# Order of work in layers 1 and 2 of a four-layer attention and expert network on one Trainium2 core

## What is computed

```python
x = x + _L1_xattn_ref(_layernorm(x), ctx_768, ...)
x = x + _L1_ffn_ref(_layernorm(x), ...)
x = x + _L2_xattn_ref(_layernorm(x), ctx_768, ...)
x = x + _L2_ffn_ref(_layernorm(x), ...)

# layer 1, attention: every linear layer rounds its input to int8 steps (by the largest value of all of it)
for Wa, ba in ((W_att0, b_att0), (W_att1, b_att1)):
    kv = bitnet_linear(image_embeds, Wa, ba)
    k = jnp.concatenate([kv, kv], axis=-1)
    scores = jnp.einsum('bse,bpe->bsp', fused, k) * inv_sqrt_e
    attn = jax.nn.softmax(scores, axis=-1)
    fused = fused + 0.1 * jnp.einsum('bsp,bpe->bse', attn, k)
h = jax.nn.relu(bitnet_linear(concatenated, W_f1, b_f1))
return bitnet_linear(h, W_f2, b_f2)

# layer 1, experts
x_attn = _layernorm(x_flat, ln_g, ln_b) @ attn_w + attn_b + x_flat
h = jax.nn.gelu(jnp.einsum('metd,edf->metf', g, w1) + b1[None, :, None, :], approximate=False)
y = jnp.einsum('metf,efd->metd', h, w2) + b2[None, :, None, :]
out = jax.nn.gelu(y @ next_w + next_b, approximate=False)

# layer 2, feed-forward, twice (forward and inverse branch)
prod = xV * jnp.cumsum(yW, axis=1)
weights = jax.nn.softmax(logits, axis=-1)
out = jnp.einsum('btkr,kdr->btd', prod * weights[..., None], U)
```

## Time and profile before

| | |
|---|---|
| median of 3 runs | 1381.35 us (1381.34 to 1382.42) |
| profiled execution | 1381.36 us, span 1379.6 us |
| TensorE busy | 1333.7 us, 97% of the span |
| VectorE, ScalarE, GpSimd busy | 975.0, 944.9, 734.8 us |
| DMA | 20.59 MB, mean 15 GB/s |

### The profile page before, as it was taken

How to read it: one execution, slowest core, us unless ns; L and a number is a source line. 1 busy time by engine, 2 the same in 40 slices (tenths; PEclk the granted TensorE clock), 3 DMA queues, 4 the chain that set the end, 5 groups by cost and what they waited for, 6 DMA issues and landing times. The chain is left out here.

```text
span 1379.6 us, 30536 instructions
## 1 busy us (share of the span) xinstructions
PE 1333.7 (97%) x10001; PEld 992.9 (72%) x10001; DVE 975.0 (71%) x2367; ACT 944.9 (68%) x1964; POOL 734.8 (53%) x787
## 2 busy tenths in 40 slices
PE   8999999998988899999999999999999999999998
PEld 6555568996556777777775787677777777777777
DVE  6776757868767677777775565777766767677783
ACT  6888877885776476766763465676766767676673
POOL 6465641204532167666657486465665656565652
PEclk9999999999999999999999999999999999999999
DMA  6300010000003100000001000000000000000003
GB/s 180 88 0 0 1 31 2 1 1 1 2 1 96 47 1 1 1 0 0 0 1 39 0 1 0 1 2 1 1 0 0 0 0 0 0 0 0 1 3 91
DMA packets 31539, 20.59 MB, mean 15 GB/s; under 512 B 9589, under 2 KB 29020, under 8 KB 31452
## 3 DMA queue, kind: packets, MB, share of 16 engines
q1 hardware_dynamic: 31224, 19.38, 5.0%
q10 hardware_dynamic: 228, 0.10, 0.0%
HBM read 18.42 MB, written 1.05 MB: 14 GB/s over the span
## 5 line engine op out<-in xcount | busy, mean ns | idle before, releaser
L2410 POOL TENSOR_TENSOR arena<-arena,l3a_rinv 128x512 f32<-128x512 f32 x256 | 259.1, 1040 | 189.1 <-DVE l3a_rinv L2822 188.8
L2713 ACT ACTIVATE arena<-l3a_scores_ps,l3a_nmax 128x512 f32<-128x512 f32 x256 | 174.9, 686 | 116.0 <-DVE l3a_nmax L2816 115.9
L2410 POOL TENSOR_TENSOR arena<-arena,l2a_rinv 128x512 f32<-128x512 f32 x128 | 129.7, 1040 | 84.9 <-DVE l2a_rinv L2822 84.2
L2816 DVE TENSOR_REDUCE l3a_nmax<-l3a_scores_ps 128x2 f32<-128x1024 f32 x128 | 155.9, 1218 | 17.7 <-PE l3a_scores_ps L2483 17.7
L904 ACT ACTIVATE l0a_prob<-l0a_scores_ps,l0a_k_scale 128x1024 f32<-128x1024 f32 x128 | 135.5, 1114 | 21.8 <-PE l0a_scores_ps L749 20.4
L2713 ACT ACTIVATE arena<-l2a_scores_ps,l2a_nmax 128x512 f32<-128x512 f32 x128 | 87.5, 686 | 57.2 <-DVE l2a_nmax L2816 57.2
L2514 PE MATMUL l3a_work_ps<-l3a_probT,l3a_v 128*64 128x256 f32 x1024 | 124.6, 385 | 0.0
L2514 PEld LDWEIGHTS l3a_work_ps<-l3a_probT,l3a_v 128*64 128x64 f32 x1024 | 67.8, 136 | 48.7 <-issue 20.0
L2816 DVE TENSOR_REDUCE l2a_nmax<-l2a_scores_ps 128x2 f32<-128x1024 f32 x64 | 77.7, 1217 | 7.4 <-PE l2a_scores_ps L2483 7.4
L2828 DVE COPY l3a_probT<-l3a_scores_ps 128x512 f32<-128x512 f32 x65 | 44.9, 690 | 44.2 <-PE l3a_scores_ps L2491 44.1
L2828 DVE COPY l3a_probT<-l3a_work_ps 128x512 f32<-128x512 f32 x63 | 43.6, 691 | 36.7 <-PE l3a_work_ps L2491 35.9
(11 more groups left out here) (805 smaller groups left out, 3731.5 us busy)
## 6 DMA issues: line engine op xcount, KB each, us to landing
l1f_w<-in_L_ffn_w SPq DMA_DIRECT2D x16, 256.0 KB, 2.8
arena<-in_ctx SPq DMA_DIRECT2D x4, 384.0 KB, 5.2
w_l_w<-in_L_ffn_W SPq DMA_DIRECT2D x1, 1024.0 KB
arena<-in_L_ffn_W SPq DMA_DIRECT2D x16, 64.0 KB, 1.9
out_x<-x_tokens SPq DMA_DIRECT2D x8, 128.0 KB, 1.9
x_tokens<-in_x SPq DMA_DIRECT2D x1, 768.0 KB, 5.9
const<-in_constants SPq DMA_DIRECT2D x1, 525.0 KB
w_l_wo<-in_L_xattn_Wo SPq DMA_DIRECT2D x1, 512.0 KB
```

The source lines that it names most:

```text
L2410: e.tensor_tensor(prob[n][:, :], prob[n][:, :], bcast(rinv[:, n:n + 1], [P, S]), ALU.mult).then_inc(m.prob_ready, 1)
L2713: e.activation(prob[at][:, :], scores_bank(b, c, u), ACT.Exp, bias=nmax[:, at:at + 1], accum_out=rsum[:, at:at + 1]).then_inc(m.exp_ready, 1)
L2816: e.tensor_reduce(nmax[:, at:at + 2], sps[:, first:first + 1024].rearrange("p (h k) -> p h k", h=2), AX.X, ALU.max, negate=True).then_inc( ...
```

## The change

Nine pieces, all of them changes of order, of waits or of the number of fillers:

- attention of layer 1: project(n+2) stands ahead of scores(n+1) in every slot from 0 on; the final projections stand behind the transposes; at the end attended(15) stands ahead of the final of batch 6; VectorE's keep_rows(1) stands ahead of the division of step 0;
- experts of layer 1: apply(0) stands ahead of quantise(2) and quantise(3); turn_z and mix wait for each tile singly; in the last turn keep_y(3, 0) stands behind update(2) and the statistics;
- layer 2: 17 fillers for 8 ahead of the softmax's transposes and 1 for 4 ahead of the last of them; norm_scales at step 5 for step 6.

```diff
@@ l1_ffn, tensor @@
             def turn_z(u):
-                e.wait_ge(m.z_ready, NT * (u + 1))
...
                 for i in range(NT):
+                    e.wait_ge(m.z_ready, NT * u + i + 1)
                     last = e.transpose(turn_ps[:, i * P:(i + 1) * P], z[u % 2][:, i, :], g.ident)
...
-                e.wait_ge(m.inner_ready, NT * (u + 1))
                 for i in range(NT):
+                    e.wait_ge(m.inner_ready, NT * u + i + 1)
                     e.matmul(mix_ps[:, i * P:(i + 1) * P], inner[u % 2][:, i, :], g.ident, start=i == 0, stop=False)
@@ l1_ffn, vector @@
             statistics(0)
+            apply(0)
             quantise(2)
             quantise(3)
-            apply(0)
...
-                keep_y(u, 0)
+                if u < TURNS - 1:
+                    keep_y(u, 0)
                 if u >= 1:
                     update(u - 1)
                     ahead.statistics(e, u - 1, next_tiles(u - 1), m.x_updated, PAIR * u)
+                if u == TURNS - 1:
+                    keep_y(u, 0)
@@ l2_ffn, tensor @@
-                keep_busy(e, g, zps, 8)
+                keep_busy(e, g, zps, 17)
...
                     if n == TURNS - 1:
-                        keep_busy(e, g, zps, 4)
+                        keep_busy(e, g, zps, 1)
@@ l2_ffn, gpsimd @@
-                        if n == 6 and u > 0:
+                        if n == 5 and u > 0:
                             norm_scales(u - 1)
@@ l1_attention, vector @@
+                    if n == -1:
+                        keep_rows(n + 2)
                     if n + 1 < STEPS:
                         invert(n + 1, 0)
-                    if n + 2 < STEPS:
+                    if n >= 0 and n + 2 < STEPS:
                         keep_rows(n + 2)
@@ l1_attention, tensor @@
                 def slot(n):
+                    if n >= 0 and n + 2 < STEPS:
+                        project(n + 2)
                     if n == 0:
-                        project(n + 2)
                         project_sum(1, 0)
                     if n + 1 < STEPS:
                         scores(n + 1)
-                    if 0 != n < STEPS - 2:
+                    if n < 0:
                         project(n + 2)
...
-                    for b in range(B):
-                        if final_slot(b) == n:
-                            final(b, 2 + sum(SUM_AT[u] <= n for u in range(2, B // 2)))
                     if n >= 0:
                         turned(n, 0)
                         turned(n, 1)
+                    for b in range(B):
+                        if final_slot(b) == n:
+                            final(b, 2 + sum(SUM_AT[u] <= n for u in range(2, B // 2)))
                     if n >= 1:
                         attended(n - 1)
...
+                attended(STEPS - 1)
                 final(B - 2, B // 2)
-                attended(STEPS - 1)
                 final(B - 1, B // 2)
```

6 lines of the change are left out of this document (3 added, 3 removed).

## The result

The changed kernel takes 1385.78 us in the median of 9 runs (1384.90 to 1387.63), the kernel before 1382.24 us in the median of 9 (1381.34 to 1384.72). The ratio is 1.0020 with a 95% interval from 1.0011 to 1.0028: the change makes the kernel slower, by 1.5 to 3.9 us. The medians lie 3.5 apart. The forecast was +1.8 us, at 1383.2; its range reached to 1386.4. The sign came out as forecast and so did the main mechanisms; the size was put too low, by about half if the medians are taken.

What follows compares the result with a forecast made beforehand. TensorE, busy nearly throughout, was taken as the bound, so only its idle time and clock count. Terms -0.4 + 3.9 - 0.5 + 0.9 - 2.1 = +1.8 on 1381.36 gave 1383.2 us, range 1379.4 to 1386.4.

Steps and rivals of the forecast that it cites:

- Start of the layer-1 experts: apply(0) ahead of two quantisings: turn_z 3.3 us late, +2.8 net, plus 1.1 for a lower clock; together +3.9.
- Rival 1: Clock stays at 1.2 GHz after the 4.6 us hole in layer-1 experts: term 5.3, sum +3.2, about 1384.8; chance 0.24.
- Layer 2, norm scales: Layer-2 experts, scales a step sooner: +1.05 in turn 1, +0.9 in turn 2, -1.1 in turn 3; together +0.9.
- Rival 3: Layer-2 term a gain: GpSimd works ahead, only turn 3 shows, -1.1 for +0.9; 1381.2, no change; chance 0.10.
- Softmax fillers: Layer-2 softmax: with no idle hole the clock stays at 2.4 GHz, -2.1; -1.0 if it falls all the same.
- Experts' end: Layer-1 experts' end: update and statistics slide into VectorE's idle hole, products' copy and transposes come sooner; -0.5.
- Attention: Layer-1 attention, all its moves together: -0.4, bounds -3.1 without the port's effect and +0.5 if late steps cost more.
- four long steps: Attention steps whose projection waits for VectorE's quantising beside GpSimd's division: 4.66 us each, +3.6 together.
- seven short steps: Attention steps with the projection first, its copy ready early: 3.50 us, 0.25 gained in each, -1.8 together.
- tail's swap: Attention's end, attended(15) ahead of final(6): swaps one short wait for another, -0.2 at most.
- Rival 2: Faster: VectorE and GpSimd run ahead, late quantisings do not hold attention's scores; attention -3.7, about 1378.5; chance 0.13.
- Rival 4: Changes in order do nothing visible, each move lying under a busy engine; 1381.4; chance 0.08.

Runs made afterwards that it cites:

- run 4: Kernel before with only the softmax fillers changed, 17 for 8 and 1 for 4; 1381.51 us, ratio 0.9986 against the kernel before.
- run 12: Kernel before, unchanged, profiled a second time; span 1382.7 us against 1379.6 in its first profile.
- run 5: Changed kernel with VectorE's quantising of image rows of batches 3 to 7 moved right behind the two maxima; 1382.09 us, ratio 0.9993 against the kernel before.
- Run 1: Changed kernel with apply(0) of the layer-1 experts put back behind quantise(2) and quantise(3); 1381.09 us, ratio 0.9990 against the kernel before.
- run 7: Changed kernel with turn_z(0) and mix(0) ahead of second_product(2) and (3), and fourteen fillers ahead of turn_z; 1383.86 us, ratio 1.0006 against the kernel before.
- run 3: Changed kernel with layer 2's norm scales at step 6 again; 1384.87 us, ratio 1.0013 against the kernel before.
- run 8: Changed kernel with the edits of Run 1 and run 2, and norm scales sooner in the last turn alone; 1376.39 us, ratio 0.9955 against the kernel before.
- run 2: Changed kernel with layer-1 attention's projections put back behind the scores; 1382.65 us, ratio 0.9995 against the kernel before.
- run 9: As run 8, but projections ahead of scores, quantising as in run 5, final of batch 6 ahead of attended(15); 1374.77 us, ratio 0.9940 against the kernel before.
- run 6: Changed kernel with quantising and shifting of image rows of batches 4 to 7 a slot sooner; 1385.29 us, ratio 1.0015 against the kernel before.

## Why the prediction came out as it did

**How the total came about.** Against the profile that the sum was made from, the change measured +3.5 for +1.8. Attention missed by +1.7, the end of the experts by +0.9, layer 2 by +0.3; the start of the experts by -0.8 and the softmax by -0.1 took some of it back, and the stages that the change does not touch gave -0.3. That the total stayed within the range owes something to misses of both signs.

**Start of the layer-1 experts, +3.9: right, and the largest term.** turn_z late by 3.3 less what mix had waited was the working, with +2.8; against starts of 11.98 (runs 4 and 12, the old order at full clock) the changed kernel's 15.88 is +3.9. turn_z itself went from 7.91 (run 12) to 12.46 after the stage's start, 4.6, of which 1.3 is the clock. Against the one profile that the sum was made from the term is +3.12, because that profile had a lower clock in the very same stretch, which the working did not take out. Behind the hole the batch products took 1.89 instead of 1.22 and the fillers 1.64 instead of 1.03: 1.3 for the clock, 1.1 was taken. Rival 1, the same course with the clock low for longer, put the term at 5.3. The profile of run 5, with this order too, comes near it: 17.05, +5.1, with the granted clock at 0.53 and 0.50 from 424.0 to 430.8, through the batch products, the fillers, turn_z and most of mix, though not the first hidden product. Both courses happen, in different executions: the five profiles with this order have 15.88, 16.31, 16.33, 16.98 and 17.05, so +3.9 to +5.1 (three of them with the clock low at the stage's start as well), and the forecast stood at their lower end. Run 1 shows that the order causes it, run 7 that it is TensorE's order against VectorE's. GpSimd's first power took 1.03 instead of 1.47 without the quantising beside it, as the working had read.

**Layer 2, norm scales, +0.9: right in each turn.** Forecast +1.05, +0.9 and -1.1; measured waits +1.00, +0.92 and -0.91, and the stage +1.22, for a sum of waits of +1.01; the other 0.2 was not traced. Rival 3, that GpSimd works ahead, falls by run 3, and run 8 has the last turn alone at -0.80, so turns 1 and 2 cost 2.0.

**Softmax fillers, -2.1: right** with 2.24, shown by run 4 with this piece alone.

**Experts' end, -0.5: right** in the stretch that it named (-0.51), wrong in what came next. "The next late thing is ScalarE's last gelu" left out the five fillers, which at a lower clock become the last thing themselves: +0.95. Run 1, with the same edit and 1.28 for the fillers, shows that it belongs to the execution, not to the edit.

**Attention, -0.4: here the sum failed;** measured +1.26, the other way. The mechanism held: four long steps of 4.73 to 4.76 (forecast 4.66), four projections waiting on quantised rows, the start -1.20 (-1.2), the hole's step -0.71 (-0.8). Four sizes were off, all one way. The long steps came to 19.01 against 15.06 of the same steps before, +3.95 for +3.6. The seven short steps became 3.54 or 3.55, the last of them 3.48, where 3.50 was taken: -1.5 for -1.8. Two steps with a final grew from 4.06 to 4.21, +0.3, which the working had at nothing; run 2 has them at 4.09, so most of it is the projection. And the tail's swap, put at "-0.2 at most", cost +0.4: run 9. "One short wait for another" was said there without adding up the chain; a bound above zero was missing. The stated upper bound for attention, +0.5, was passed.

**Slips of arithmetic in the record**, none of them large: 4 x 4.66 less 15.1 is +3.5, not +3.6; the upper bound for attention comes to +0.4; rival 1's +3.2 gives 1384.6, not 1384.8.

**Rival 2** (VectorE and GpSimd run ahead, the quantisings do not hold) falls: with the change four projections wait for quantised rows, 4.4 us in all, and without their move (run 2) or with the quantising elsewhere (run 5) the long steps go. **Rival 4** falls with the table.

**The argument on the clock was weak.** "After 1.92 of idle it fell, after the 2.36 hole it did not" was read as a property of the two holes; run 12 shows the 2.36 hole with a fall. One profile shows one draw. The time of the kernel before was also read from its luckiest side: 1381.36 was among the fastest of what became nine runs with a median of 1382.24. Taken against that median the forecast rise of 1.8 would have stood at 1384.0, with 1385.78 measured. The ratio came out right at the bound of 0.2%, beyond which the forecast had given 0.33.

How much of a run's time is this draw can be read from the mean granted clock of each timing. Of 30 timings of the kernel before beside runs 1 to 4, the eleven with 0.998 took 1381.06 to 1382.34 us, median 1381.48; the seven with 0.995 took 1383.65 to 1385.18. The six of the changed kernel with 0.998 took 1384.90 to 1386.77, median 1385.67. At the same mean clock, then, the change costs about 4.2 us, a little more than the medians of all timings say; the two sets come from different sessions.

What stays open: how often each hole lets the clock fall. Fourteen profiles show that it varies, not how it is distributed; behind the 4.7 hole there was a fall in all five of its profiles (the changed kernel, runs 2, 3, 5 and 6).
